# Expert tiles turned by DRAM and VectorE instead of TensorE, slot weights stored and loaded as a row

## The reference

```python
x = x + 0.5 * ffn(layernorm(x))
x = x + attention(layernorm(x))
x = x + 0.5 * ffn(layernorm(x))

def ffn(x):                                    # 8 experts, the best 2 for each token
    probs = softmax(x @ gate_w + gate_b, over tokens)
    vals, idx = top_k(probs, 2)
    y = relu(relu(relu(x @ w1 + b1) @ w2 + b2) @ w3 + b3)      # for each expert, 256 wide
    w_tok = one_hot(idx) weighted by vals
    v = einsum('ebso,bse->eo', y, w_tok)       # one vector of 256 for each expert
    return ind @ v                             # ind: which experts a token chose
```

## Time and profile before

| | us |
|---|---|
| median of three runs | 2123.17 (2122.85 to 2123.97) |
| the profiled execution | 2125.24 |
| its span, first to last instruction | 2123.5 |
| TensorE, VectorE, ScalarE, GpSimd busy | 2046.4, 1820.4, 1600.1, 416.1 |
| tiles of pass 0 | about 69 to 287 |
| tiles of pass 1 | about 1886 to 2104 |

### The profile page before, as it was taken

How to read it: one execution, slowest core, us unless ns; L and a number is a source line. 1 busy time by engine, 2 the same in 40 slices (tenths; PEclk the granted TensorE clock), 3 DMA queues, 4 the chain that set the end, 5 groups by cost and what they waited for, 6 DMA issues and landing times.

```text
span 2123.5 us, 99873 instructions
## 1 busy us (share of the span) xinstructions
PE 2046.4 (96%) x43655; PEld 1587.4 (75%) x43659; DVE 1820.4 (86%) x4031; ACT 1600.1 (75%) x3315; POOL 416.1 (20%) x1118
## 2 busy tenths in 40 slices
PE   5899989999999999999999999999999999979998
PEld 3788866377778777777777777777777776758885
DVE  6666666899999999999999999999999994766665
ACT  5244446599999999999999999999999998424442
POOL 1333303411121111111111111111121111023330
PEclk8799989999999999999999999999999999979998
DMA  8211103400010000100001001000010001231112
GB/s 273 73 47 45 47 16 117 142 30 24 14 33 12 27 28 10 34 17 21 31 7 34 22 17 33 9 30 24 14 34 13 26 5 51 72 118 49 42 50 87
DMA packets 70394, 94.36 MB, mean 44 GB/s; under 512 B 16640, under 2 KB 59396, under 8 KB 69956
## 3 DMA queue, kind: packets, MB, share of 16 engines
q1 hardware_dynamic: 62796, 68.75, 10.1%
q0 software_dynamic: 6816, 19.20, 3.4%
q10 hardware_dynamic: 344, 0.01, 0.0%
HBM read 62.24 MB, written 25.43 MB: 41 GB/s over the span
## 4 chain that ended last, share of the span: by engine, by line
PE 89%; DVE 5%; issue 2%; ACT 1%; POOL 1%; SPq 1%; DMA 0%; another core or an unknown queue 0%; ACTq 0%; DVEq 0%; POOLq 0%
PE bank L1257 39%; PE bank L1250 22%; PE bank L1132 17%; PE bank L1339 3%; PE bank L1143 1%; PE bank L1367 1%; PE bank L1300 1%; PE bank L1150 1%; DVE stats L1397 1%; PE bank L1021 1%; SPq L698 0%; POOL work L591 0%; DVE work L1586 0%; PE bank L1210 0%; PE bank L1307 0%
## 5 line engine op out<-in xcount | busy, mean ns | idle before, releaser
L964 ACT ACTIVATE feat<-bank 128x512 f32<-128x512 f32 (+3 forms) x2304 | 1263.4, 565 | 112.9 <-PE bank L1257 12.6
L1257 PE MATMUL bank<-work 96*32 96x512 bf16 (+2 forms) x15872 | 1207.0, 370 | 5.1 <-DVE work L1764 3.8
L1764 DVE TENSOR_REDUCE work<-bank 128x1 f32<-128x512 f32 (+1 forms) x1920 | 1179.9, 661 | 25.7 <-PE bank L1257 22.9
L1250 PE MATMUL bank<-feat,phase 128*17 128x128 f32 (+3 forms) x18432 | 881.4, 263 | 0.3 <-ACT feat L970 0.3
L1250 PEld LDWEIGHTS bank<-feat,phase 128*17 128x17 f32 x18432 | 592.4, 98 | 267.0 <-ACT feat L970 13.8
L1257 PEld LDWEIGHTS bank<-work 96*32 96x32 bf16 (+1 forms) x15872 | 475.0, 96 | 56.7 <-DVE work L1764 24.3
L1132 PE MATMUL bank<-work 128*128 128x256 f32 (+1 forms) x1872 | 399.1, 364 | 4.2 <-issue 2.9
L1132 PEld LDWEIGHTS bank<-work 128*128 128x128 f32 x1872 | 325.5, 192 | 41.0 <-issue 4.4
L625 POOL TENSOR_SCALAR_AFFINE_SELECT feat<-feat 128x128 f32<-128x128 f32 x512 | 146.1, 295 | 455.0 <-ACT feat L964 438.6
L1648 DVE COPY work<-phase 128x514 f32 x234 | 101.6, 436 | 124.8 <-ACT work L878 101.0
L578 POOL DMA_INDIRECT work<-token_table,row_no x142 | 138.1, 973 | 302.7 <-PE bank L1143 145.5
(11 more groups left out here) (201 smaller groups left out, 1379.2 us busy)
## 6 DMA issues: line engine op xcount, KB each, us to landing
phase<-in_w SPq DMA_DIRECT2D x12, 1024.0 KB, 12.0
work<-qk_parts SPq DMA_DIRECT2D x60, 192.0 KB
token_table<-rows SPq DMA_DIRECT2D x8, 1056.0 KB, 8.7
work<-work SPq DMA_DIRECT2D x512, 0.5 KB
qk_parts<-phase SPq DMA_DIRECT2D x20, 384.0 KB, 2.7
work<-qk_parts SPq DMA_DIRECT2D x60, 128.0 KB
qk_parts<-work SPq DMA_DIRECT2D x12, 384.0 KB, 2.6
x_res<-in_x SPq DMA_DIRECT2D x8, 512.0 KB
```

The source lines that it names most:

```text
L964: eng.activation(p_ring[:, n % P_RING, lo:QB], s_bank("probs", n)[:, lo:QB], ACT.Exp, scale=HD ** -0.5).then_inc(sig.s_done, 1)
L1250: mm = eng.matmul(bank[ACC_BANK][GRID * g:GRID * g + VW, GRID * i0:P], v_aug[:, t, h, :], weights[:, i0:TPJ, g, :], start=(t == 0), stop=( ...
L1257: mm = eng.matmul(out[GRID * g:GRID * (g + 1), width], left[:, GRID * g:GRID * (g + 1)], right, start=start, stop=stop)
L1764: eng.tensor_reduce(maxima[:, h % 2, j, PLACE[i], at:at + 1], scores[:, 0:hi - lo], AX_X, ALU.max).then_inc(sig.a_done, 1)
```

## The change

From tile 4 on (`DIRECT` = 4), TensorE no longer turns the tile. SyncE stores each gathered sub-tile to DRAM, and reads it back with four DMAs, one for each group of 32 partitions, in 128-byte pieces placed so that every 32x32 block stands where it belongs, not yet turned inside. VectorE turns the blocks with one transpose instruction straight into the input of the first layer (`turn_tile`). This runs on a ring of two (`TURN_RING`) in the memory of `rows`. Tiles 0 to 3 go as before.

For all tiles, the weight column is widened to 32 columns (`GRID`) and not 128, and VectorE turns its blocks. ScalarE stores the result to DRAM, and a step later loads one 128-byte piece for each block of 32 slots to all 128 partitions. TensorE's weight transposes and ScalarE's copy from bank 1 go. The first layer's input is now laid out sub-tile by sub-tile.

```diff
 load_tile (GpSimd):
-                need.wait_ge(sig.xt[f], KD * subs_before(j - NXG + 1))
-                need.wait_ge(sig.w_col[f], 3 * (j - NXG + 1))
+                if j - NXG < DIRECT:
+                    need.wait_ge(sig.xt[f], KD * subs_before(j - NXG + 1))
+                else:
+                    need.wait_ge(sig.slot_stored[j % NXG], 16 * stored_uses(f, j - NXG))
+                need.wait_ge(sig.w_col[f], 4 * (j - NXG + 1))
 SyncE:
+            def store_slots(f, j):
+                for u, n in enumerate(SUBS[j]):
+                    need.wait_ge(sig.slot[j % NXG][u], 16 * slot_uses(f, j, u))
+                    eng.dma_start(slots_dram[f][n].rearrange("k p f -> p k f"),
+                                  x_slot[:, j % NXG, u, 0:D].rearrange("p (k f) -> p k f", k=KD),
+                                  ).then_inc(sig.slot_stored[j % NXG], 16)
+            def load_to_turn(f, j):
+                n = len(SUBS[j])
+                tile = slots_dram[f][SUBS[j][0]:SUBS[j][0] + n]
+                need.wait_ge(sig.slot_stored[j % NXG], 16 * stored_uses(f, j))
+                need.wait_ge(sig.table[f], 16 * GROUPS)
+                need.wait_ge(sig.tile_turned[f], j - TURN_RING - DIRECT + 1)
+                for a in range(P // GRID):
+                    eng.dma_start(to_turn[GRID * a:GRID * (a + 1), j % TURN_RING, 0:n * D].rearrange(
+                        "p (u f) -> p u f", f=GRID),
+                        tile[:, :, :, GRID * a:GRID * (a + 1)].rearrange("u k (b r) f -> r (u k b) f", r=GRID),
+                        ).then_inc(sig.turn_loaded[j % TURN_RING], 16)
+            def tiles(f):                      # runs behind store_table(f)
+                for j in range(DIRECT, N_TILES):
+                    store_slots(f, j)
+                    if j > DIRECT:
+                        load_to_turn(f, j - 1)
+                load_to_turn(f, LAST)
 ScalarE, in step n behind the first relu of tile n-1: load_weight(f, n - 1), store_weight(f, n)
+            def store_weight(f, j):
+                need.wait_ge(sig.w_col[f], 4 * (j + 1))
+                eng.dma_start(weights_dram[f][subs].rearrange("u p s -> p u s"),
+                              w_turned[:, j % 2, 0:len(SUBS[j])]).then_inc(sig.w_stored[j % 2], 16)
+            def load_weight(f, j):
+                need.wait_ge(sig.w_stored[j % 2], ...)
+                need.wait_ge(sig.weighted[f], KD * (j - W_RING + 1))
+                blocks = weights_dram[f][subs].rearrange("u (b o) s -> (u b) o s", o=GRID)[:, 0, :]
+                eng.dma_start(w_row[:, j % W_RING, 0:WIDTH[j]].rearrange("p (c s) -> p c s", s=GRID),
+                              blocks.unsqueeze(0).to_broadcast([P, WIDTH[j] // GRID, GRID])
+                              ).then_inc(sig.w_loaded[j % 2], 16)
 copy_tile (ScalarE) and transpose_tile (TensorE): only for j < DIRECT; transpose_weight is gone
 layer 0 (TensorE):
+                    need.wait_ge(sig.tile_turned[f], j - DIRECT + 1)
 VectorE, widen_weight:
-                eng.tensor_copy(w_wide[:, b, 0:n], bc(w_col[:, b, 0:n], 2, [P, n, P]))
+                eng.tensor_copy(w_wide[:, b, 0:n], bc(w_col[:, b, 0:n], 2, [P, n, GRID]))
+                need.wait_ge(sig.w_col[f], 4 * j + 3)
+                need.wait_ge(sig.w_stored[b], ...)             # of tile j-2
+                eng.transpose(w_turned[:, b, 0:n], w_wide[:, b, 0:n])
 VectorE, in step j >= DIRECT between stage(f, j, 1) and stage(f, j + 1, 0):
+            def turn_tile(f, j):
+                need.wait_ge(sig.turn_loaded[j % TURN_RING], 16 * (P // GRID) * turn_uses(f, j))
+                need.wait_ge(sig.layer[f][0], j - 1)
+                eng.transpose(acts_in[:, j % 2, 0:KD * WIDTH[j]],
+                              to_turn[:, j % TURN_RING, 0:KD * WIDTH[j]]).then_inc(sig.tile_turned[f], 1)
 weigh (VectorE):
-                need.wait_ge(sig.w_row[f], j + 1)
+                need.wait_ge(sig.w_loaded[j % 2], ...)
```

More of the change, by code:

```diff
@@ L256, in slot_uses, with stored_uses, turn_uses @@
     return f * len(fills) + sum(n <= j for n in fills)
+def stored_uses(f, j):
+    fills = [n for n in range(DIRECT, N_TILES) if n % NXG == j % NXG]
+    return f * sum(len(SUBS[n]) for n in fills) + sum(len(SUBS[n]) for n in fills if n <= j)
+def turn_uses(f, j):
+    fills = [n for n in range(DIRECT, N_TILES) if n % TURN_RING == j % TURN_RING]
+    return f * len(fills) + sum(n <= j for n in fills)
 class Waits:
@@ L352, in macaron_block @@
         table = [nc.dram_tensor(f"token_table{f}", (S + 1, ROW), F32).ap() for f in range(2)]
+        slots_dram = [nc.dram_tensor(f"tile_rows{f}", (N_SUB, KD, P, P), F32).ap() for f in range(2)]
+        weights_dram = [nc.dram_tensor(f"slot_weights{f}", (N_SUB, P, GRID), F32).ap() for f in range(2)]
         parts_dram = nc.dram_tensor("qk_parts", (2, 3, D, S), BF16).ap()
@@ L461, in macaron_block @@
         heads = rows[:, :, 0:D]
+        to_turn = rows[:, :, :].rearrange("p i r -> p (i r)")[:, 0:TURN_RING * TS * D].rearrange(
+            "p (b s) -> p b s", b=TURN_RING)
         def bc(ap, axis, shape):
@@ L708, in _ @@
             store_table(0)
+            tiles(0)
             for n in range(EARLY_CHUNKS):
@@ L735, in _ @@
             store_table(1)
+            tiles(1)
             for i0, i1 in zip(STORES, STORES[1:]):
@@ L861, in copy_tile @@
                     return
[L862 to L867, removed]
-                need.wait_ge(sig.weighted[f], KD * (j - W_RING + 1))
-                eng.activation(w_row[:, j % W_RING, 0:WIDTH[j]], bank[1][:, 0:WIDTH[j]],
-                               ACT.Copy).then_inc(sig.w_row[f], 1)
+                if j < DIRECT:
+                    need.wait_ge(sig.xt[f], KD * subs_before(j + 1))
+                    need.wait_ge(sig.layer[f][0], j - 1)
+                    eng.activation(acts_in[:, j % 2, 0:KD * WIDTH[j]], bank[0][:, 0:KD * WIDTH[j]],
+                                   ACT.Copy).then_inc(sig.xt_copy[f], 1)
+            def store_weight(f, j):
+                if j >= N_TILES:
+                    return
+                need.wait_ge(sig.w_col[f], 4 * (j + 1))
+                subs = slice(SUBS[j][0], SUBS[j][0] + len(SUBS[j]))
+                eng.dma_start(weights_dram[f][subs].rearrange("u p s -> p u s"),
+                              w_turned[:, j % 2, 0:len(SUBS[j])]).then_inc(sig.w_stored[j % 2], 16)
+            def load_weight(f, j):
+                if not 0 <= j < N_TILES:
+                    return
+                need.wait_ge(sig.w_stored[j % 2], 16 * (f * len(range(j % 2, N_TILES, 2)) + j // 2 + 1))
+                need.wait_ge(sig.weighted[f], KD * (j - W_RING + 1))
+                need.wait_ge(sig.w_loaded[j % 2], 16 * (f * len(range(j % 2, N_TILES, 2)) + j // 2))
+                subs = slice(SUBS[j][0], SUBS[j][0] + len(SUBS[j]))
+                blocks = weights_dram[f][subs].rearrange("u (b o) s -> (u b) o s", o=GRID)[:, 0, :]
+                eng.dma_start(w_row[:, j % W_RING, 0:WIDTH[j]].rearrange("p (c s) -> p c s", s=GRID),
+                              blocks.unsqueeze(0).to_broadcast([P, WIDTH[j] // GRID, GRID])).then_inc(sig.w_loaded[j % 2], 16)
             def relu_first(f, j):
@@ L1117, in layer @@
                 if l == 0:
[L1118 removed]
+                    need.wait_ge(sig.xt_copy[f], min(j + 1, DIRECT))
+                    need.wait_ge(sig.tile_turned[f], j - DIRECT + 1)
                     if j != LAST:
@@ L1142, in transpose_tile @@
                     for k in range(KD):
-                        eng.transpose(bank[0][:, k * TILE + u * P:k * TILE + (u + 1) * P],
+                        eng.transpose(bank[0][:, (u * KD + k) * P:(u * KD + k + 1) * P],
                                       x_slot[:, j % NXG, u, k * P:(k + 1) * P], ident[:, :]).then_inc(sig.xt[f], 1)
[L1146 to L1151, removed]
             def tiles(f):
```

39 lines of the change are left out of this document (28 added, 11 removed).

## The result

| | us | ratio to before, 95% interval |
|---|---|---|
| before | 2123.01 (2122.8 to 2123.97) | |
| after | 2313.46 (2309.72 to 2317.72) | 1.0897 (1.0877 to 1.0916) |

The forecast was 2088 with a range of 2079 to 2175. The profiled execution of the changed kernel has a span of 2311.9 us. First the page: engines, the chain that ended last by engine and by line, and the two new transposes of VectorE.

What follows compares the result with a forecast made beforehand. TensorE's matmul work was taken to bound the kernel: 43.2 us of transposes saved, less 6 and 2 given back, is 35 us; profiled 2125.24 minus 35 is 2090, which less 2.1 over the median gives 2088, range 2079 to 2175.

Steps and rivals of the forecast that it cites:

- the transfers themselves: DMA per wide tile: 128-byte pieces at 13 ns, 512-byte at 28.5; 4.63 us of a 5.19 us step, 89%.
- TensorE's side: TensorE loses its tile and weight transposes, 0.65 us per wide tile from number 4 on, 43.2 us over two passes.
- The 6 and 2 us that the sum gave back: 6 us for VectorE exceeding TensorE in narrow-layer steps (bounds 0 and 12); 2 us for ramps and tail (0 and 6).
- VectorE's side: VectorE's step becomes 4.84 us, under TensorE's 5.19 by 0.35; transposes 0.24 and 0.70 us, widening copy about 0.19.
- Rival 1: VectorE becomes the bound if the 512-column turn costs 1.21 us: wide step 5.35 us, time 2112 us; chance 0.09.
- The tile's chain: Gather, two stores and four loads take 13.3 us, needed after 22 us; loads land with 2.5 us of cover.
- ScalarE's side: DMA issues of 1.2 us replace 0.96 of copies, costing nothing; weight-store wait has some 5 us, landing takes 2.7.
- Rival 2: From tile 4 on, dear small pieces (over 18.8 ns) make DMA engines set the step: 2165 to 2252 us; chance 0.22.
- rival 3: Chains too long for one step ahead: loads over 2.5 us late or ScalarE blocked at weight store; 2105 to 2128; chance 0.09.

Runs made afterwards that it cites:

- four-DMA control: Changed kernel with the weight row loaded by four DMAs of 32 partitions, every partition still reading row 0 of each block: 2387.50 us, ratio 1.1311.
- the three good variants: Changed kernel with weight row read from 32 equal rows (0.9861 repeated), as one row in 1 KB pieces (0.9874 repeated), or the latter plus gather ring of four (0.9886).

## Why the prediction was wrong

**The step that failed** is "the transfers themselves", in its term for the weight row: 1024 pieces x 13 ns / 16 = 0.8 us of engine time, with the landing put at 2.7 us and called covered. It took 6.0 us. The price of 13 ns was right: 11.6 to 12.9 ns is what the profile books for such a piece, slow or fast. Wrong was to take the booked time for all the time from one piece of an engine to its next. In the earlier trace rows the small pieces came from as many places as there were pieces; here 1024 reads go to eight blocks that lie 4 KB apart, they come 6 ns apart, and what they wait for is not in the busy share. The 6 us then held the next weight store, and with it VectorE, ScalarE and the other queues.

**TensorE's side** was right. With the tile turn alone the step fell by the 0.43 us of the earlier trace rows; with both parts and a spread load, 30 us were gained (0.9861 x 2123 = 2093) against 35 forecast. The 6 and 2 us that the sum gave back were not measured one by one.

**VectorE's side** was right to 0.01 us in its prices. The three new or changed instructions, from the run with one 1 KB row, 88 to 265 us:

```profile
L1738 DVE STREAM_TRANSPOSE work<-rows 128x512 f32<-128x512 f32 x29 | 20.5, 705 | 5.8 <-DMA rows<-tile_rows 5.6 <-issue 0.2
L1732 DVE STREAM_TRANSPOSE work<-work 128x64 f32<-128x64 f32 x28 | 6.9, 245 | 1.0
L1729 DVE COPY work<-work 128x64 f32<-128x64 f32 x28 | 5.5, 195 | 1.0
```

0.70, 0.24 and 0.19 had been worked out from the earlier trace rows. Rival 1 was not seen.

**The tile's chain** of gather, store, load and turn had its cover but for a few us: from 88 to 265 us the turn waited 3.6 us for its loads in the kernel with the spread load (0.4 when repeated), and 9.9 and 5.6 us in that with one 1 KB row. In the kernel with the spread load SyncE's packets were booked 47.6% x 150 x 16 / 72517 = 15.8 ns each, where my prices make (2048 x 13 + 512 x 28.5)/2560 = 16.1 (by size 12.9 ns for its 128-byte and 28.3 ns for its 512-byte packets), and 84 to 86% of the engines were booked (89% forecast).

**ScalarE's side** was wrong in what it waited for. I named the wait for the store of a step before and covered it with 2.7 us; I did not ask what stands in the same queue ahead of that store.

**Rival 2** had the sign, the place (DMA) and even the remark that 128 partitions read the same eight blocks, but priced all small pieces alike, from 18.8 ns booked a piece. Its mechanism is refuted: booked time never rose. What was to tell it from rival 3, ns per packet, told nothing: it stood at 11.6 in the slow load. Read from different places, ScalarE's 128-byte pieces were booked 19.1% x 150 x 16 / 36286 = 12.6 ns each. The Trainium skill (DMA: Bandwidth & Descriptors, Specifications) asks for 512 bytes or more for line rate, with read-modify-write below. The trace agrees that a 128-byte piece runs below the rate of a large one, about 10 bytes per ns of an engine against 21 for 1 KB in 49.8 ns; it is not as dear as a large one, and the threshold does not tell the slow load from the fast one. Rival 3 described how the harm shows, ScalarE standing at the weight store's semaphore, but not its size, for it had only crowding as its cause.

The largest gain seen is 1.5% (1.4% when repeated), from the change as made with the load spread over 32 rows; the three good variants can't be told apart.

## What to carry to other kernels

Before a broadcast from DRAM is called cheap, look at the addresses of its pieces, how often each is read and how far apart they lie, and read it in pieces as long as can be, or from copies: here eight blocks 4 KB apart, read 128 times each, took 6 us, and the same bytes in 1 KB pieces 2 us, which held up nothing. An engine's busy share can't show such a transfer; packets per microsecond can, in a stretch where only that transfer runs. For a transfer that something waits for, ask what was issued ahead of it on the same queue.

## What the runs showed that was not expected

Whole loads of 1024 pieces of 128 bytes took 5.7 to 6.0 us from 8 DRAM blocks 4 KB apart (6.9 in the four-DMA control), 3.4 us from 32 blocks and 2.1 us from 256; a narrow tile's 512 pieces from 4 such blocks took 2.3 to 2.5 us. In the slow ones from 8 blocks ScalarE's queue was booked for 12 to 13% of the engines' time. While such a load drained, the two other queues moved 9 packets in 3.5 us. Whether the reads wait in memory or in the engines, and whether for the same block or for the 4 KB distance, was not tried.
